# A causal attention and routed feed-forward kernel: the last projection split by heads, and the first group's queries loaded ahead of its keys

## The reference

```
xn    = layernorm(x)
q, k  = rope(split_heads(xn @ Wq.T)), rope(split_heads(xn @ Wk.T))     # 16 heads of 16
v     = split_heads(xn @ Wv.T)
probs = softmax(where(causal, q k^T / 4, -1e9))
attn  = (probs @ v) joined @ Wo.T
m     = 3-tap mix of xn along the sequence
h     = m @ W1[p] + b1[p];  paths = h @ W2[p] + b2[p]   (9 paths)
idx   = argmax(tanh(m @ Wo1 + bo1) @ Wo2 + bo2)         (one path per row)
out   = x + attn + layernorm(xn + paths[idx]) * gamma + beta
```

## Time and profile before

| | us |
|---|---|
| median of 3 runs | 783.17 (782.35 to 784.49) |
| the profiled execution | 784.09 |
| its span, first to last instruction | 782.4 |
| PE busy | 739.9 (95%) |
| DVE busy | 641.7 (82%) |
| ACT busy | 448.9 (57%) |
| POOL busy | 288.3 (37%) |

### The profile page before, as it was taken

The page is one execution under the profiler, slowest core; times in us unless marked ns, Lnnn a source line. Parts: engine busy times, 40 slices in busy tenths (PEclk is TensorE's granted clock), DMA queues, the critical chain, the costliest instruction groups (busy, mean ns, idle before and its releaser), DMA issues.

```text
span 782.4 us, 12591 instructions
## 1 busy us (share of the span) xinstructions
PE 739.9 (95%) x4416; PEld 372.3 (48%) x4416; DVE 641.7 (82%) x1894; ACT 448.9 (57%) x780; POOL 288.3 (37%) x459
## 2 busy tenths in 40 slices
PE   4869999999999999999999999999999999999996
PEld 2432344354565544345465544445465554354544
DVE  5989999889798789888988789897988669878622
ACT  2262645765655654775656655666657555754672
POOL 2001123990615112893514213695334203130623
PEclk9965999999999999999999999999999999999999
DMA  7259050224613434112651615111560705100103
GB/s 242 97 164 191 8 114 2 72 81 113 105 15 59 105 91 77 53 60 83 118 72 28 136 56 112 33 69 53 122 109 2 136 28 112 33 2 2 28 1 81
DMA packets 40577, 59.98 MB, mean 77 GB/s; under 512 B 4813, under 2 KB 36830, under 8 KB 37634
## 3 DMA queue, kind: packets, MB, share of 16 engines
q1 hardware_dynamic: 36002, 54.39, 29.4%
q0 software_dynamic: 4224, 4.19, 4.1%
q10 hardware_dynamic: 288, 0.59, 0.2%
HBM read 42.04 MB, written 16.85 MB: 75 GB/s over the span
## 4 chain that ended last, share of the span: by engine, by line
PE 71%; POOL 10%; DVE 8%; ACT 6%; DMA 2%; issue 1%; SPq 1%; POOLq 0%; ACTq 0%; DVEq 0%
PE bank L1557 14%; PE bank L1538 14%; PE bank L1519 14%; PE bank L1500 7%; PE bank L1510 6%; PE bank L1462 3%; POOL prob L1014 3%; PE bank L1585 3%; PE bank L1473 3%; ACT prob L1132 3%; POOL raw L993 2%; POOL turned L991 2%; PE bank L1480 2%; PE bank L1567 2%; POOL turned L999 1%
## 5 line engine op out<-in xcount | busy, mean ns | idle before, releaser
L1132 ACT ACTIVATE prob<-bank 128x512 f32<-128x512 f32 x576 | 324.6, 597 | 194.4 <-PE bank L1538 191.3
L1350 DVE CUSTOM_DVE_ANT_0 bank<-bank,causal_sb 128x384 f32<-128x384 f32 (+3 forms) x512 | 240.3, 513 | 34.3 <-PE bank L1519 33.5
L1519 PE MATMUL bank<-k_st,q_st 96*128 96x512 bf16 (+3 forms) x768 | 236.1, 339 | 8.4 <-DMA q_st<-scratch 4.0
L1014 POOL TENSOR_SCALAR_AFFINE_SELECT prob<-prob 128x256 f32<-128x256 f32 (+1 forms) x320 | 125.9, 427 | 294.0 <-ACT prob L1132 291.1
L1538 PE MATMUL bank<-q_st,k_st 98*128 98x512 bf16 (+3 forms) x768 | 212.4, 331 | 7.9 <-ACT prob L1132 5.8
L1353 DVE TENSOR_REDUCE piecemax<-bank 128x1 f32<-128x512 f32 x256 | 164.0, 683 | 18.6 <-PE bank L1519 18.2
L1557 PE MATMUL bank<-prob,v_sb 128*17 128x512 f32 (+3 forms) x1536 | 143.9, 495 | 0.8 <-POOL prob L1014 0.8
L1519 PEld LDWEIGHTS bank<-k_st,q_st 96*128 96x128 bf16 x768 | 72.4, 98 | 130.8 <-DVE piecemax L1350 49.4
L1538 PEld LDWEIGHTS bank<-q_st,k_st 98*128 98x128 bf16 x768 | 70.0, 98 | 113.7 <-ACT prob L1132 56.7
L1510 PE MATMUL bank<-w_sb,mid 128*128 128x256 f32 (+1 forms) x320 | 83.7, 383 | 0.0
L1462 PE MATMUL bank<-xnT,wqk_sb 128*128 128x512 f32 x128 | 68.3, 639 | 4.6 <-ACT xnT L1079 3.7
(11 more groups left out here) (82 smaller groups left out, 698.7 us busy)
## 6 DMA issues: line engine op xcount, KB each, us to landing
scratch<-parts SPq DMA_DIRECT2D x16, 768.0 KB, 3.8
q_st<-scratch SPq DMA_DIRECT2D x90, 128.0 KB, 6.8
k_st<-scratch SPq DMA_DIRECT2D x15, 384.0 KB, 4.6
z<-in_x SPq DMA_DIRECT2D x8, 512.0 KB, 4.5
mask<-chosen SPq DMA_DIRECT2D x16, 256.0 KB
z<-in_x POOLq DMA_DIRECT2D x8, 512.0 KB, 6.7
out<-z SPq DMA_DIRECT2D x8, 512.0 KB, 4.7
k_st<-scratch SPq DMA_DIRECT2D x15, 256.0 KB, 5.4
```

Source lines behind the costliest of these rows:

```text
L1014: nc.gpsimd.affine_select(out=d, in_=d, compare_op=ALU.is_ge, fill=0.0, base=0, pattern=pattern, channel_multiplier=-1).then_inc(masked, 1)
L1132: nc.scalar.activation(prob[:, place_of(G, i), :], ps[:, :], ACT.Exp, scale=float(DK) ** -0.5).then_inc(act_took, 1)
L1350: nc.vector.tensor_tensor_reduce(ps, ps, causal_sb[:, HALF - w:HALF], 1.0, NEG, ALU.add, ALU.max, to).then_inc(dve_took, 1)
L1519: nc.tensor.matmul(begin(("max", G, u))[:, 0:w], q_st[0:PARTS, G % STACKS, h, t * P:(t + 1) * P], k_st[0:PARTS, G % STACKS, h, k0:k0 + w], ...
```

## The change

The change has four parts.

1. The values of the first half of batch 0 (v units 0 and 1) are computed before the q and k projections of the second half instead of after them, and wait only for the turned x of their own half.
2. For group 0, the six q DMAs of each half are issued as soon as q is stored, ahead of the three k DMAs. In the second half they have a semaphore of their own, and the sixteen old-key `max` units wait for q alone. These sixteen are put ahead of the sixteen diagonal ones. The `place` of the first half of group 0 is issued by ACT instead of SP, and `set_ones` for stacks 1 and 2 moves from after the values to the start of ACT's stream.
3. The planner's inputs change, and with them the order of the first group and of what is threaded into it and into groups 1 and 2. From the middle of group 1 on, up to the last steps of group 15, the order is as before.
4. The last projection (batch 3, second half) is no longer two units of two row tiles but four units `endproj` of one row tile. Chunk 0 of `attnT` (heads 0 to 7) is turned before pv step 7 of group 15, and its four products stand before the last group's sums are turned; only chunk 1 is left behind them. The result goes out in two DMAs of two row tiles.

The core of the diff:

```diff
@@ prologue
     head("fill", 0, 0)
+    for i in range(2):
+        head("v", 0, i)
     project(0, 1)
...
+    head("qfill", 0, 1)
     head("fill", 0, 1)
-    for i in range(4):
+    for i in range(2, 4):
         head("v", 0, i)
@@ plan
-        units = range(len(FIRST_UNITS), NM) if G == 0 else range(NM)
+        units = sorted(range(len(FIRST_UNITS), NM), key=has_diagonal) if G == 0 else range(NM)
...
-            at = a + (e - a) * (u - units[0]) / len(units)
+            at = a + (e - a) * units.index(u) / len(units)
...
+            end = (n, half) == (B - 1, 1)
             for c in range(NC):
-                add(e + 0.03 * c, "attnT", n, c, half)
-            for i in range(2):
+                add(e + 0.03 * c - (0.17 if end and c == 0 else 0), "attnT", n, c, half)
+            for i in range(HT if end else 0):
+                add(e - 0.13 + 0.01 * i, "part", 0, "endproj", i)
+                add(e + 0.09 + 0.02 * i, "endproj", i)
+            for i in range(0 if end else 2):
                 unit_at(e + 0.09 + 0.08 * i, 0.04, "proj", n, half, i)
@@ bank_choice
+    if at >= NG * B - 0.4 and what != "S":
+        return (3, 4, 5, 6, 7)
@@ needs
         G, u = a
-        first = [("fill", G, 0)] + ([("fill", 0, 1)] if G == 0 and MAX_UNITS[u][0] >= HT else [])
+        first = [("fill", G, 0)]
+        if G == 0 and MAX_UNITS[u][0] >= HT:
+            first.append(("fill" if has_diagonal(u) else "qfill", 0, 1))
@@ SP: fill
+                elif half == 0:
+                    sp.wait_ge(parts_stored[0][0], 16)
+                    fill_q(0, 0, HALF, stack_filled[0])
+                    sp.wait_ge(parts_stored[1][0], 16)
+                    fill_k(0, 0, HALF, stack_filled[0])
+                else:
+                    sp.wait_ge(parts_stored[1][1], 16)
+                    fill_k(0, HALF, S, second_filled)
+
+            def fill_second_q():
+                sp.wait_ge(parts_stored[0][1], 16)
+                fill_q(0, HALF, S, second_q_filled)
@@ SP: store_out
+                for i in range(2):
+                    sp.wait_ge(dve_took, TOOK["endproj", 2 * i + 1])
+                    a = half * HALF + 2 * i * P
+                    t = half * HT + 2 * i
+                    eng.dma_start(out[n, a:a + 2 * P, :].rearrange("(t p) d -> p t d", p=P),
+                                  z[:, n % 2, t:t + 2, :]).then_inc(out_stored[n % 2][half], 16)
@@ ACT
+            def place_shift(G, half):
+                act.wait_ge(act_took, TOOK["shift", G, half])
+                a, e = half * HALF, (half + 1) * HALF
+                for k in range(SHIFT):
+                    eng.dma_start(q_st[PARTS + k:PARTS + k + 1, G % STACKS, :, a:e],
+                                  shiftT[k * GH:(k + 1) * GH, a:e]).then_inc(shift_placed[half], 16)
...
             set_ones(0)
+            set_ones(1)
...
+                    if name == ("xnT", 0, 0, 0):
+                        set_ones(2)
@@ PE: max_scores
                 if G == 0 and t >= HT:
-                    pe.wait_ge(second_filled, 16 * FILL_DMAS)
+                    pe.wait_ge(second_q_filled, 16 * Q_DMAS)
+                    if has_diagonal(u):
+                        pe.wait_ge(second_filled, 16 * (FILL_DMAS - Q_DMAS))
@@ PE: the last projection
+            def end_project(c, i):
+
+                if c == 0:
+                    pe.wait_ge(act_took, TOOK["attnT", B - 1, 0, 1])
+                else:
+                    pe.wait_ge(dve_took, TOOK["attnT", B - 1, 1, 1])
+                ps = begin(("endproj", i), c)
+                return nc.tensor.matmul(ps[:, 0:D], attnT[:, c, i * P:(i + 1) * P], wo_sb[:, c, :],
+                                        start=(c == 0), stop=(c == NC - 1))
```

More of the change, by code:

```diff
@@ L323, in bank_choice, with groups_before @@
         return (1, 2, 6, 7)
+    if at >= NG * B - 0.4 and what != "S":
+        return (3, 4, 5, 6, 7)
     return {"S": (1, 2), "max": (3, 4, 5)}.get(what, (6, 7))
+def groups_before(n, c, half):
+    return range(c * NG // NC, (c + 1) * NG // NC) if (n, half) == (B - 1, 1) else range(NG)
 def former(n, qk, half):
@@ L337, in needs @@
     what, a = name[0], name[1:]
+    if what == "part" and a[1] == "endproj":
+        return [("attnT", B - 1, 0, 1)], []
     if what == "part":
@@ L381, in needs @@
             first.append(("S", G - STACKS, NS - 1))
+    elif what == "qfill":
+        first = [("store", 0, 0, 1)]
     elif what == "v":
-        n, _ = a
-        first = [("xnT", n, c, 1) for c in range(NC)]
+        n, i = a
+        first = [("xnT", n, c, i // 2) for c in range(NC)]
         then = [("pv", NG * (n - 1) - 1, NSTEPS - 1)] if n >= 2 else []
@@ L434, in needs @@
         n, c, half = a
-        first = [("oT", NG * n + g, half) for g in range(NG)]
+        first = [("oT", NG * n + g, half) for g in groups_before(n, c, half)]
         then = [("rope", min(n + 1, B - 1), 0, 1)]
@@ L442, in needs @@
         then = [("addx", n, half)]
+    elif what == "endproj":
+        first = [("attnT", B - 1, c, 1) for c in range(NC)]
+        then = [("addx", B - 1, 1)]
     elif what == "out":
-        first = [("proj", *a, 1)]
+        first = [("endproj", HT - 1) if tuple(a) == (B - 1, 1) else ("proj", *a, 1)]
     elif what == "max":
         G, u = a
-        first = [("fill", G, 0)] + ([("fill", 0, 1)] if G == 0 and MAX_UNITS[u][0] >= HT else [])
+        first = [("fill", G, 0)]
+        if G == 0 and MAX_UNITS[u][0] >= HT:
+            first.append(("fill" if has_diagonal(u) else "qfill", 0, 1))
         then = [("cut", G - 2, 1)] if G >= 2 else []
@@ L488 @@
              "pool": ("pow", "turn", "sel", "scale", "affine", "addx"),
-             "dma": ("load", "store", "fill", "keep", "spread", "place", "out")}
+             "dma": ("load", "store", "fill", "qfill", "keep", "spread", "place", "out")}
 ENGINE_OF = {what: e for e, names in BY_ENGINE.items() for what in names}
-PE_US = {"xnT": 0.44, "qk": 0.86, "v": 0.86, "early": 0.86, "mid": 0.86, "paths": 0.86, "proj": 0.86, "scores": 1.0,
+PE_US = {"xnT": 0.44, "qk": 0.86, "v": 0.86, "early": 0.86, "mid": 0.86, "paths": 0.86, "proj": 0.86, "endproj": 0.43, "scores": 1.0,
          "onehot": 0.45, "S": 0.22, "shift": 0.25, "oT": 0.44, "attnT": 0.44}
@@ new lines, in stack_source, with fill_q, fill_k @@
+            def stack_source(G, qk, a, e):
+                n, g = divmod(G, NG)
+                return scratch[n, qk].rearrange("a e (r h) t -> (a e r) h t", h=H)[:, g * GH:(g + 1) * GH, a:e]
+            def fill_q(G, a, e, done):
+                st, src = q_st[:, G % STACKS, :, a:e], stack_source(G, 0, a, e)
+                for k, part in enumerate(Q_PARTS):
+                    eng.dma_start(st[k * DK:(k + 1) * DK], src[part * DK:(part + 1) * DK]).then_inc(done, 16)
+            def fill_k(G, a, e, done):
+                st, src = k_st[:, G % STACKS, :, a:e], stack_source(G, 1, a, e)
+                for row, first, rows in ((0, 0, 3 * DK), (3 * DK, 0, 2 * DK), (5 * DK, 0, DK)):
+                    eng.dma_start(st[row:row + rows], src[first:first + rows]).then_inc(done, 16)
@@ L942, in _ @@
                     fill(*name[1:])
+                elif what == "qfill":
+                    fill_second_q()
                 elif what == "keep":
@@ L1433, in _ @@
                     copy_attnT(*name[1:])
+                elif what == "endproj":
+                    finish_end(name[1])
                 elif what == "proj":
```

67 lines of the change are left out of this document (35 added, 32 removed).

## The result

The changed kernel takes 786.67 us (median of seven runs, 785.75 to 788.61); the kernel before, on the same chip, 783.17 (seven runs, 782.35 to 785.81). The ratio is 1.004, with a 95% interval of 1.0024 to 1.0057. The forecast was 780.6, range 777.3 to 783.0. So the sign was wrong, and the time lies outside the range. The profiled execution of the changed kernel took 785.75 us with a span of 783.9.

What follows compares the result with a forecast made beforehand. PE was taken to bound the middle, DVE beside a half-clock PE the start, and a serial thread the end. Terms -0.7 + 0 + 0.4 - 2.3 = -2.6 took 783.17 to 780.6 us, range 777.3 to 783.0.

Steps and rivals of the forecast that it cites:

- Step (2): Second half's fill and first half's place: first old-key unit about 52.7 us, first S unit about 55.3; DVE wait 0.7, before 1.49.
- Steps (3) and (4): First group's new order at half clock: DVE idle 4.3 us as before, worth 0 with the fill; then `early` block +0.4 us.
- The sum: Whole kernel: -0.7 + 0 + 0.4 - 2.3 = -2.6 us, giving 780.6, with PEclk 0.50 from 57 to 70 us.
- rival A: S and old-key stretch: the clock rises about 62 us, 2.3 us off the forecast, 778.3 us; chance 0.25.
- rival C: Second half's S units begin 1.3 us later, PE at half clock until `early`; 6.1 us slower, 786.7 us; chance 0.1.
- parts 2 and 3: The fill and the first group's new order: together worth 0 us, between -2.3 and +1.3.
- parts 1 to 4: The start: values in the gap -0.7 us, fill and first group's order 0, `early` block +0.4.
- the prediction's own sign: Wrong if the start up to 110 us gains or loses more than 2.5 us, or the tail gains less than 1.
- Step (1): Values in PE's gap before the second qk block: DVE's 0.65 us wait goes, everything on DVE moves up, -0.7 us.
- Step (5): The tail from the last pv steps: fewer transposes and projection records, shorter add and DMA; -2.3 us, between -1.0 and -3.0.
- the last DMA: At the end of the tail: it carries half the bytes, -0.3 us, an estimate between 0 and -0.6.

Runs made afterwards that it cites:

- removing it in two ways: Changed kernel with the place of group 0's first half back on SP: 781.60 us; or still on ACT, with SP holding group 1's fill until it lands: 782.02 us.
- half a dose: Changed kernel, place on ACT, group 1's three k transfers issued at once and its six q transfers held until the place landed: 784.07 us, ratio 1.0009.
- the place mended: Changed kernel with only the place of group 0's first half issued by SP again, ahead of group 1's fill: 781.60 us, ratio 0.9982.
- the end part alone: Kernel before with only the new last projection (four units of one tile, heads 0 to 7 ahead, two output DMAs): 779.97 us, ratio 0.9965.
- the last padded kernel: Changed kernel, place on SP, overwritten PE products ahead of the first group's sixteen second-half diagonal units and group 1's first 21 max units: 780.50 us, ratio 0.9961.
- The shorter padding: Changed kernel, place on SP, overwritten PE products ahead of the first group's sixteen second-half diagonal units only: 782.08 us, ratio 0.9985.

## Why the prediction was wrong

**Step (2), the second paragraph: this is the step that failed.** "The place of the first half no longer stands behind the fill on SP at 54.88 but goes out from ACT at about 52.7, so the first S unit can start at about 55.3 ... On SP the fills of groups 1 and 2 start some 5 us earlier and nothing is late by it." The issue times were right, and so was the paragraph before it: the first old-key maximum reached DVE at 52.60, though the six q issues took 3.67 us from 46.29 on and not 2.78. The landing of the place was not: I gave the place the 2.6 us that it took in the kernel before, from SP's issue at 54.88 to the S unit at 57.52, when the fill of group 1 was issued behind it, from 56.30. I did not ask what SP would put into the same DMA engines in those microseconds. The fill of group 1 is 1.5 MB (three k transfers of 384, 256 and 128 KB and six q transfers of 128 KB). Before, SP's order guarded the place: it was issued ahead of that fill. On ACT it lost that guard: SP issued the three k transfers of group 1 before 52.8 us, and the six q transfers from 52.83 on, beside the place. It landed 6.54 us after its issue, and the S unit, which in the new order stands ahead of most old-key units, held PE and DVE for 5 us. Price: 4.5 us by the ratios (1.0040 against 0.9982), shown by removing it in two ways and by half a dose. The Trainium skill states in "DMA: Bandwidth & Descriptors", section "Issuing engines are not separate DMA queues", that transfers started by different engines run on the same 16 DMA engines and interleave there. I did not weigh it. The traces here agree: the place issued by ACT took 6.54 us beside SP's fill and 1.8 us without it.

**Steps (3) and (4), the clock.** The sum said that the clock stays at 0.50 from 57 to 70 us. It rose at 64.5, in the dense stretch of S and old-key units, as rival A had it. In all nine kernels with the new order it rose between 59.0 and 67.8 us, in the five with the old order between 77.2 and 81.5. The Trainium skill's rule weighed in the prediction ("TensorE: Matmul & The Clock Gate", section "What's actually happening"), that activity releases the throttled state, agrees with these rises. My row was not what I took it for: the old stretch had 128 and 256 wide units between the 512 wide ones, and PE was busy 4.95, 4.87 and 4.85 of 5 us from 60 to 75 us, not for eight us only, without a rise; why, no run tells. But rival A stopped at the rise. PE, faster than DVE, ran into gaps and fell back at 74.7 us, and it was at half clock until 95.2, which is rival C's second half: "the clock stays at 0.50 beyond about 92 us". The `early` block, +0.4 in the sum, cost about 1.7 (four of its eight records at 0.85 us). A and C were put as alternatives; what happened is A's rise followed by C's cost. With the place mended, this leaves the kernel 1.6 us above the end part alone by the medians, 1.3 by the ratios; that most of it is the half clock is supported by the last padded kernel, not settled.

The sum's own currency failed there too. It priced parts 2 and 3 by DVE's idle time, 4.3 us as before. With the place on SP, DVE idles only 0.6 us from 55 to 85 us, where it idled 4.3 in the kernel before, and the kernel is not faster by it: PE is the later of the two by then, DVE idles 3.3 us from 90 to 100 us, and group 1's first S unit starts 2.1 us later than before (109.65 against 107.54). At group 3 it is 1.2 us behind the kernel before, where parts 1 to 4 were forecast 0.3 ahead. Three of its stretches:

```profile
60.00:65.00 5.00, 4.46 (x30) 1.77 (x28) 5.00 (x14) 3.30 (x7) 2.73 (x7) 0.98 1.02 172
...
90.00:95.00 5.00, 5.00 (x30) 1.81 (x28) 3.21 (x17) 3.92 (x7) 2.02 (x2) 0.91 0.00 0
95.00:100.00 5.00, 4.90 (x33) 2.70 (x28) 3.50 (x15) 3.18 (x7) 0.00 (x0) 1.00 0.01 3
```

A small slip beside it: nine pairs of 0.86 us less half a pair are 7.3 us, not 7.2. By the prediction's own sign, more than 2.5 us lost up to 110 us, it was wrong at the start: 6.4 us at group 1's first S unit.

**Step (1)** was right in its mechanism: v at 23.73 us in the gap, the second qk block not later, and DVE waits for nothing at 33 us. The rows for the earlier trace rows:

```profile
23.73 3.69 PE L1550 MATMUL bank<-wv_sb,xnT 128*128 128x256 f32 x16 [0.64 <-DVE raw L1324]
...
27.73 6.71 PE L1539 MATMUL bank<-xnT,wqk_sb 128*128 128x512 f32 x15 [0.30 <-ACT xnT L1139]
```

The first shift is 0.66 us earlier, forecast 0.7. Whether it arrives at the end, the runs cannot tell.

**Step (5)**, the tail, was right within 0.2 us in every term but one, and -2.3 was a little small: -2.5 by the two profiles, -3.2 by the medians of the end part alone (-2.7 by its ratio, interval -3.8 to -1.8 us). The term that was off is the last DMA, put at 0.3 with 0.6 as its bound and worked out from no row: from its issue to the end of the span are 3.5 us before (778.93 to 782.4), and 2.6 from the second issue now, so 0.8.

**Rival C** gave 786.7, the very time, with a chance of 0.1, but by another mechanism: its 6.1 us were all clock and a 1.3 us delay. That the number came out is luck. The largest piece, the 4.5 us of the place, was in no rival.

## What to carry to other kernels

A small transfer that something waits for must be issued ahead of the large ones, in time, not only in its own engine's stream. Moving it to another engine takes it out of the order that protected it, so ask what every other issuer sends in the microseconds around it, and take its landing time from a moment when that much is queued. And in a stretch that two engines pace by turns, an engine that gets ahead can pay for it later: here PE's early work left gaps, and the next block that needed PE found it at half clock.

## What the runs showed of the hardware

- A 4 KB transfer landed 1.8 us after its issue with the next group's fill held back, 4.4 us with 0.75 MB of that fill issued ahead, 6.5 and 8.0 us with all of its 1.5 MB issued ahead and beside, and more from 55.8 us on. The DMA engines' busy share was 1.02 and 1.00 then. That it was issued by another engine did not bring it past them; its packets did not start before 56.9 us, 4.2 us after ACT began to issue.
- PE work whose results are thrown away made the kernel no slower in three cases, and in one of them 1.6 us faster, with the granted clock at 1.00 (2.4 GHz) from 59 to 96 us instead of falling to 0.50 (1.2 GHz) at 70. That one had the most of it: 24,064 columns, an estimate of 10 us at the 0.22 us that 512 columns take at full clock. The shorter padding had 10,240 columns, by the same estimate 4.4 us and not the 7 that its expectation says.
- Stretches of 3.4 us at half clock appear in the middle of some executions, at full load, and not in others: at 281.5 us in the profile before, at 281.0 to 289.7 in four others, and once at 463.8. One is worth about 1.5 us: the changed kernel's units are 5.5 us behind the kernel before at groups 3 and 4 and 4.0 from group 5 on. Two single profiles differ by as much as a whole part of this change.
